# A layer of a Trainium2 kernel: projecting one batch's tokens at a time, normalising along the free axis, then transposing, in place of projecting head by head and summing squares with matmuls

## The reference, cut to what matters

```python
def _rmsnorm(x, w):
    var = jnp.mean(xf * xf, axis=-1, keepdims=True)
    return (xf * jax.lax.rsqrt(var + EPS)).astype(x.dtype) * w
q = (hidden_states @ Wq.T).reshape(bsz, q_len, H, HD).transpose(0, 2, 1, 3)
k = (cross_attention_states @ Wk.T).reshape(bsz, kv_len, KVH, HD).transpose(0, 2, 1, 3)
v = (cross_attention_states @ Wv.T).reshape(bsz, kv_len, KVH, HD).transpose(0, 2, 1, 3)
q = _rmsnorm(q, q_norm_w)
...
k = _rmsnorm(k, k_norm_w)
scores = jnp.einsum('bhqd,bhkd->bhqk', q, k) * scale
scores = scores + attention_mask[:, :, :, :kv_len]
probs = jax.nn.softmax(scores.astype(jnp.float32), axis=-1).astype(q.dtype)
out = jnp.einsum('bhqk,bhkd->bhqd', probs, v)
return out @ Wo.T
```

## Time and profile before

| | us |
|---|---|
| median of 3 runs (1788.86 to 1794.28) | 1790.83 |
| the profiled execution's own time | 1788.83 |
| its span, first to last instruction | 1787.0 |
| busy in the span: PE / DVE / POOL / ACT | 1642.3 / 1172.7 / 1053.3 / 811.2 |

### The profile page before, as it was taken

One profiled execution on the slowest core, in us unless ns is written; L12 is line 12 of the kernel. 1 busy time (PEld: TensorE's weight loads), 2 busy tenths in 40 slices (PEclk: granted clock), 3 DMA queues, 4 the chain that ended last, 5 costly groups with the idle time before them and its releaser, 6 DMA issues. The chain is left out here.

```text
span 1787.0 us, 26495 instructions
## 1 busy us (share of the span) xinstructions
PE 1642.3 (92%) x8578; PEld 1366.5 (76%) x8578; DVE 1172.7 (66%) x2367; ACT 811.2 (45%) x2584; POOL 1053.3 (59%) x1090
## 2 busy tenths in 40 slices
PE   6499974899999999999999999999999999996896
PEld 5377852688888888887888788888888888885684
DVE  4277757477777777666778765565755556555684
ACT  4297822344444444443444444444544444443442
POOL 6544411466666778665667676555766676653362
PEclk9699986999999999999999999999999999999895
DMA  6532100222222222212112231222222322220100
GB/s 214 148 67 45 43 1 11 66 65 66 65 60 60 72 73 77 55 57 60 53 54 69 69 95 60 62 63 59 75 74 82 84 78 80 80 66 8 59 25 24
DMA packets 73705, 117.22 MB, mean 66 GB/s; under 512 B 9633, under 2 KB 21281, under 8 KB 73569
## 3 DMA queue, kind: packets, MB, share of 16 engines
q1 hardware_dynamic: 73344, 115.26, 22.6%
q10 hardware_dynamic: 224, 0.26, 0.1%
HBM read 108.15 MB, written 7.34 MB: 65 GB/s over the span
## 5 line engine op out<-in xcount | busy, mean ns | idle before, releaser
L1156 POOL TENSOR_TENSOR a_probs<-a_probs,a_total 128x512 f32<-128x512 f32 x128 | 135.3, 1057 | 210.1 <-DVE a_total L1580 208.9
L62 POOL TENSOR_TENSOR a_w_lo<-k_ring,a_w_hi 128x512 fp32r<-128x512 f32 x186 | 240.5, 1293 | 14.9
L47 PE MATMUL ps<-a_wo_hi,a_oT_lo 128*128 128x512 f32 x512 | 211.9, 414 | 5.5 <-DVE a_oT_lo L62 3.9
L47 PE MATMUL ps<-k_xT_hi,a_w_lo 128*128 128x512 f32 x512 | 204.7, 400 | 5.6 <-DVE a_w_lo L62 5.6
L49 PE MATMUL ps<-k_xT_hi,a_w_hi 128*128 128x512 f32 x512 | 203.8, 398 | 0.0
L48 PE MATMUL ps<-k_xT_lo,a_w_hi 128*128 128x512 f32 x512 | 203.7, 398 | 0.0
L49 PE MATMUL ps<-a_wo_hi,a_oT_hi 128*128 128x512 f32 x512 | 201.1, 393 | 0.0
L48 PE MATMUL ps<-a_wo_lo,a_oT_hi 128*128 128x512 f32 x512 | 199.6, 390 | 0.0
L1417 ACT ACTIVATE a_v_hi<-ps 128x128 fp32r<-128x128 f32 x128 | 35.5, 278 | 359.2 <-PE ps L1265 359.2
L62 POOL TENSOR_TENSOR a_wo_lo<-k_ring,a_wo_hi 128x512 fp32r<-128x512 f32 x128 | 165.5, 1293 | 10.2
L1555 DVE TENSOR_TENSOR a_cross<-ps,a_cross 128x512 f32<-128x512 f32 x128 | 88.1, 688 | 120.0 <-ACT a_cross L1403 117.5
(11 more groups left out here) (398 smaller groups left out, 4598.0 us busy)
## 6 DMA issues: line engine op xcount, KB each, us to landing
k_ring<-in_L_wq SPq DMA_DIRECT2D x132, 256.0 KB, 2.6
k_ring<-in_L_wo SPq DMA_DIRECT2D x128, 256.0 KB, 2.6
k_ring<-in_L_wkv SPq DMA_DIRECT2D x66, 256.0 KB, 2.6
h_q_stack<-q_part SPq DMA_DIRECT2D x24, 256.0 KB, 4.3
k_ring<-in_L_main SPq DMA_DIRECT2D x12, 256.0 KB, 3.1
p_c_raw<-in_cT SPq DMA_DIRECT2D x4, 512.0 KB, 5.6
x<-in_x SPq DMA_DIRECT2D x8, 256.0 KB, 7.8
q_part<-p_part_hi SPq DMA_DIRECT2D x8, 256.0 KB, 2.6
```

What stands on the lines that cost most here:

```text
L47: pe.matmul(out, lhs_lo, rhs_hi, start=start, stop=False)
L62: return eng.tensor_tensor(out_lo, value, hi.bitcast(F32), ALU.subtract)
L1156: pool.tensor_tensor(heads(probs[:, :]), heads(probs[:, :]), along_last(total[:, :], S), ALU.mult).then_inc(s["probs"], 1)
```

## The change

L1 projects **rows**: one batch's 128 tokens at a time, with the tokens as the stationary operand and the weights as the moving one. `project_rows(m)` does 12 matmuls of 512 columns (the four query heads of the group, into one bank of PSUM) and 12 of 256 columns (value and key head, into half a bank). The sum of squares is then along the free axis. ACT squares key and queries at once (640 columns), DVE sums them to five numbers a token and adds epsilon, POOL takes the power of 128x5, DVE multiplies the five heads by their scales, and PE turns the five heads (`turn_heads`), from where ACT and DVE split them for the score matmuls. The values come out with tokens on the partitions, so `values` and its transpose go for L1. `sums`, the spreading matmul, `add_mask` and the rest of the cross-partition norm go. The mask is added to one part of the scores by a single DVE instruction (`mask_scores`), which takes the place of ACT's copy of that part (`take_cross`).

L1's rows run three steps ahead of the items (ROW_LOOK); the loops begin at step -3. A unit's weights stay for its four rows: the Q chunks live in `qT`, which L1 no longer needs for queries, and K and V come interleaved in two chunks kept in a weight ring of five places. All six first chunks are split by ACT and DVE at step -3. L2 keeps its old form; its first eight heads are projected in steps 61 to 65 (`projects_of_step`). The second half of the feed-forward layer begins one step later. The values have three buffers in place of two. The weights are laid out for this on the host, and a DMA scratch size of 1024 is asked for.

The core of the diff (left out: names, semaphores, places of tiles, waits on freed places, the shift of L2's counters):

```diff
+def projects_of_step(T):
+
+    first = LAYER_ITEMS
+    early = {first - 3: (0, 1), first - 2: (2, 3), first - 1: (4, 5), first: (6,), first + 1: (7,)}
+    if T in early:
+        return [first + n for n in early[T]]
+    return [T + LOOK] if first + 1 < T < ITEMS - LOOK else []
...
+    if r == 0:
+        before, after = [("K", v + 1, 1), ("O", v, 2)], [("O", v, 3)]
+    elif r == 1:
+        before, after = [("Q", v + 2, 0), ("Q", v + 2, 1)], []
+    elif r == 2:
+        before, after = [("Q", v + 2, 2), ("Q", v + 2, 3)], []
+    else:
+        before, after = [("K", v + 2, 0), ("O", v + 1, 0), ("O", v + 1, 1)], []
...
+    between = {
+        57: ([("K", first, 0)], []), 58: ([("Q", first, 0)], [("Q", first, 1)]),
+        59: ([("O", last, 0)], [("O", last, 1)]), 60: ([("O", last, 2)], [("O", last, 3)]),
+        61: ([], [("Q", first, 2), ("Q", first, 3)]), 62: ([("V", first, 0)], [("K", second, 0), ("Q", second, 0)]),
+        63: ([("Q", second, 1), ("O", first, 0)], [("O", first, 1)]), 64: ([("Q", second, 2), ("O", first, 2)], [("O", first, 3)]),
+        65: ([("Q", second, 3), ("V", second, 0)], [("K", second + 1, 0)])}
...
+    extra = {21: [("S", 0, 0)], 22: [("U", 0, 0)], 29: [("M", 0, 0), ("M", 0, 1)], 30: [("M", 0, 2)], 31: [("M", 0, 3)],
+             61: [("M", 1, 0)], 62: [("M", 1, 1)], 63: [("M", 1, 2)], 64: [("M", 1, 3)]}
...
+            def row_scales(m):
+                pool.wait_ge(s["veps"], m + 1)
+                pool.tensor_tensor(scales[:, :], scales[:, :], C.neg_half[:, 0:HEADS], ALU.pow).then_inc(s["scale"], 1)
...
+            for T in range(START, ITEMS + 1):
+                if is_row(T + 2):
+                    row_scales(T + 2)
...
-                if 0 <= P - 1 < LAYER_ITEMS:
-                    if (P - 1) % HQ == 0:
-                        key_scales((P - 1) // HQ)
-                    query_scales(P - 1)
                 if is_item(T + 1):
                     normalise(T + 1)
                 for c in after:
...
+            def project_rows(m):
+
+                u, j = m // UNIT, m % UNIT
+                rows_x = [tuple(head(x, j) for x in pair) for pair in tokens(R_[half_of(u)])]
+                rows_c = [tuple(head(x, j) for x in pair) for pair in context_tokens(half_of(u))]
+                wait_from_one(pe, s["normed"], m)
+                for k in range(KT):
+                    if j == 0:
+                        chunk_ready(pe, ("Q", u, k))
+                    last = matmul_split(pe, bank_q, rows_x[k], home(("Q", u, k)), k == 0, k == KT - 1)
+                last.then_inc(s["q_mm"], 1)
+                wait_from_one(pe, s["kT_lo"], m)
+                for k in range(KT):
+                    if j == 0 and k % 2 == 0:
+                        chunk_ready(pe, ("K", u, k // 2))
+                    both = tuple(head(x, k % 2, VK) for x in home(("K", u, k // 2)))
+                    last = matmul_split(pe, bank_vk, rows_c[k], both, k == 0, k == KT - 1)
+                last.then_inc(s["vk_mm"], 1)
+
+            def turn_heads(m):
+
+                pe.wait_ge(s["normed"], m + 1)
+                wait_from_one(pe, s["pT_lo"], m - 1)
+                pe.wait_ge(s["v_lo"], m + 1)
+                for h in range(HQ):
+                    pe.transpose(head(bank_pT, h), head(rows, 1 + h), C.ident[:, :])
+                pe.transpose(bank_kT, head(rows, 0), C.ident[:, :]).then_inc(s["turned"], 1)
...
+            for t in range(START, ITEMS + 1):
                 if is_item(t + 1):
                     scores(t + 1)
                 if is_item(t):
                     turn(t)
                 if is_item(t - 1):
                     project_out(t - 1)
-                if 0 <= P - 1 < LAYER_ITEMS:
-                    sums(P - 1, t + 1)
-                if is_item(t + 1):
+                if is_item(t + 1) and not normed(t + 1):
                     values(t + 1)
                 if is_item(t):
                     mix(t)
-                if is_item(P):
+                if is_row(t + 2):
+                    turn_heads(t + 2)
+                if is_row(t + 3):
+                    project_rows(t + 3)
+                for P in projects_of_step(t):
                     project(P)
...
+            def square_rows(m):
+
+                act.wait_ge(s["q_mm"], m + 1)
+                act.wait_ge(s["vk_mm"], m + 1)
+                wait_from_one(act, s["turned"], m)
+                act.activation(rows[:, :], bank_rows, ACT.Square).then_inc(s["squares"], 1)
+
+            def round_queries(m):
+                act.activation(q_item[m % 2][0][:, :], bank_pT, ACT.Copy).then_inc(s["q_hi"], 1)
...
+            def sum_squares(m):
+
+                dve.wait_ge(s["squares"], m + 1)
+                dve.tensor_reduce(scales[:, :], by_head(rows[:, :]), AX.X, ALU.add).then_inc(s["square_sum"], 1)
+                dve.wait_ge(s["square_sum"], m + 1)
+                dve.tensor_scalar(scales[:, :], scales[:, :], HD * QK_EPS, None, ALU.add).then_inc(s["veps"], 1)
+
+            def scale_rows(m):
+
+                dve.wait_ge(s["scale"], m + 1)
+                dve.wait_ge(s["v_lo"], m + 1)
+                dve.tensor_tensor(by_head(rows[:, :]), by_head(bank_rows), along_last(scales[:, :], HD), ALU.mult).then_inc(s["normed"], 1)
...
+                if is_row(t + 2):
+                    sum_squares(t + 2)
                 if is_item(t + 1):
-                    sum_scores(t + 1)
+                    if normed(t + 1):
+                        mask_scores(t + 1)
+                    else:
+                        sum_scores(t + 1)
                 if is_item(t):
                     split_pT(t)
+                if is_row(t + 2):
+                    low_values(t + 2)
+                    scale_rows(t + 2)
                 if is_item(t + 1):
                     if normed(t + 1):
-                        add_mask(t + 1)
+                        sum_scores(t + 1)
                     maximum(t + 1)
...
+                if is_row(t + 2):
+                    low_keys(t + 2)
+                    low_queries(t + 2)
                 if is_item(t + 1):
                     invert(t + 1)
```

More of the change, by code:

```diff
@@ L939, in chunks_of_step @@
         before, after = [("Q", v + 2, 2), ("O", v + 1, 0)], [("O", v + 1, 1)]
[L940 to L948 removed]
+    columns_first = [[c for c in part if 0 <= c[1] < UNITS] for part in (before, after)]
+    first, second = last + 1, last + 2
+    between = {
[4 more added lines that the diff above has]
+        65: ([("Q", second, 3), ("V", second, 0)], [("K", second + 1, 0)])}
+    before, after = between[T] if T in between else rows_first if T < LAYER_ITEMS else columns_first
+    before, after = list(before), list(after)
+    extra = {21: [("S", 0, 0)], 22: [("U", 0, 0)], 29: [("M", 0, 0), ("M", 0, 1)], 30: [("M", 0, 2)], 31: [("M", 0, 3)],
+             61: [("M", 1, 0)], 62: [("M", 1, 1)], 63: [("M", 1, 2)], 64: [("M", 1, 3)]}
+    after += extra.get(T, [])
     if T in (97, 99, 101, 103):
```

367 lines of the change are left out of this document (167 added, 200 removed).

## The result

The changed kernel takes 1729.12 us (median of 4 runs, 1727.99 to 1734.99), the kernel before 1792.55 us beside it (4 runs, 1788.86 to 1799.53). The ratio is 0.9645, with a 95% interval of 0.9625 to 0.9665. A second set of runs gave 1730.55 us and 0.9638 (0.9611 to 0.9665). The forecast was 1742, in a range of 1727 to 1774: right in direction and mechanism, and 11 to 13 us too slow.

What follows compares the result with a forecast made beforehand. The prediction took PE's own instructions to bound L1. From the profiled 1788.8 us, - 53 - 12 + 4 + 3 + 9 = 1740, plus 2.0 for the median, gave 1742 us, range 1727 to 1774 (forecast's own 1727 to 1757).

Steps and rivals of the forecast that it cites:

- The bound: L1 is bound by PE's own instructions: PE busy 314 of 320 us; forecast with PE still the bound, chance 0.62.
- 38.5 to 39.5: Sign in the changed profile: units of L1 without feed-forward pieces lie this many us apart.
- PE's work, -53: PE in L1: 5.35 us a unit leave, 2.0 come, net 3.3 less in 16 units, 53 us less.
- dear 256 columns: Rival, PE's row projections: a 256-column matmul costs 0.17 us, giving 1780 us; chance 0.05.
- transposes in series: Rival, PE's five transposes a row: they don't overlap, 1.1 us more each row, giving 1812 us; chance 0.02.
- The chain under PE: Row's norm, from projection's end (T0) to scaled rows: done 0.2 to 0.6 us before PE reaches `turn_heads` at 4.83.
- Waits that go, -12: PE's waits in L1 at `turn`, `project_out` and `sums`, caused by late DVE masking, go: 12 us less.
- The start, +4 (0 to +10): Start of L1: PE waits 4.2, 3.3 and about 2 us at the first three `turn_heads`, net 4 us more.
- The seam, +3: Seam to L2, step 62: second query head waits 1.5 us for its bank; with its like elsewhere, 3 us more.
- Late steps, +9: Eight to ten steps with feed-forward pieces or extra chunks: POOL's power or DVE's reduction 1 to 2 us late.
- The rivals that ended slower than before (0.07): POOL late with the power in every step, 1826 us, chance 0.05; transposes that don't overlap, 1812 us, chance 0.02.

Runs made afterwards that it cites:

- e_turns_twice: The changed kernel with the five transposes of an item's heads done twice into the same places: 1763.37 us, ratio 0.9839.
- e_one_mask_before: The kernel before with one VectorE instruction adding the mask in place of four that scale by the query's factor and add it: 1782.51 us, ratio 0.9932.
- e_power_twice: The changed kernel with GpSimd doing the power of an item's five sums twice, first into a spare tile: 1770.56 us, ratio 0.9876.
- e_delay128: The changed kernel with a VectorE copy of 128 columns put ahead of the scaling of an item's rows: 1734.09 us, ratio 0.9678.
- e_power_late: The changed kernel with GpSimd's power put behind the first weight chunk of its step instead of ahead of it: 1756.59 us, ratio 0.9791.
- e_fewer_sums: The kernel before with fewer, four-column matmuls for the norm's sums and a spreading matmul of 128 columns instead of 512: 1755.14 us, ratio 0.9782.

## Why the prediction was right, and by which terms it was off

**The bound.** Right. PE is busy 279 of 280 us, and the transposes that e_turns_twice adds to PE alone come through in full. The unit, 38.05 us, lies a little below the 38.5 to 39.5 that the prediction gave as its sign; its own step of 9.58 makes 38.3.

**PE's work, -53.** Right in its net, by two errors that cancel. A unit of the changed kernel is 38.05 us with next to no waits, one of before without its waits 41.44 (e_one_mask_before): 3.4 us a unit, forecast 3.3. I had read `scores` as 0.93 us from one step. In the changed kernel they take 0.86 (508.62 to 509.48), and they did in many steps of before: my unit of 41.7 was 0.3 too long, and my step of 9.58 0.07 too long. Five transposes (0.46 for 0.45) and twelve matmuls of 256 columns (4 x 0.36 = 1.44) came out as priced; the rivals of dear 256 columns and of transposes in series fall with that.

**The chain under PE.** Right step by step: squares 0.24 behind T0 (0.20), the reduction at 0.97 (0.95, given as 1.0), the power at 2.08 (2.1), scaled at 4.3 (4.1 to 4.5), slack 0.43 (0.2 to 0.6; the prediction's own 4.83 less 4.1 to 4.5 is 0.3 to 0.7, from which it must have taken a hand-over of 0.1); e_power_twice and e_delay128 bear out a slack of some 0.4.

**Waits that go, -12.** Right: 12 us in e_one_mask_before (8.8 by its marks), of which its trace shows 7 as waits from 380 us on; in the changed kernel none of the 12.5 us of before in that stretch is left, and 3.3 of other kinds have come.

**The start, +4 (0 to +10).** Right, a little small. The waits inside the start, from the second matmul group to the first `mix`, are 2.4 + 5.0 + 3.2 + 1.8 + 0.2 = 12.5 us. Before had 2.4 + 1.5, two of 0.3 and 0.5 for weights, and these two, together 7.0:

```profile
326.01 1.05 PE L1230 MATMUL ps<-ones,a_squares 128*128 128x1 f32 x8 [1.18 <-ACT a_squares L1392]
332.01 1.05 PE L1230 MATMUL ps<-ones,a_squares 128*128 128x1 f32 x8 [1.18 <-ACT a_squares L1392]
```

That is +5.5 in waits. The lower granted clock of the start (0.75 for 0.89) comes on top, and no run prices it. For the first three `turn_heads` I had 4.2, 3.3 and 2; they are 5.0, 3.2 and 0.2, so that part holds. What I had left out is the 2.4 us before the second group of weights is there and the 1.8 us of the first `mix`; on the side of before I had counted 5.4 for 7.0.

**The seam, +3.** One wait of 1.66 us at 977.53, as worked out (1.5); its likes did not come.

**Late steps, +9.** This is the term that failed. I supposed eight to ten steps in which extra chunks or feed-forward pieces make POOL's power or VectorE's reduction 1 to 2 us late. The trace has 1.0 us of such waits in three places. The reason is in the rows: GpSimd stands idle 2.4 us ahead of the power in half of the steps of a plain unit, and a step with feed-forward pieces is longer on PE too, so that the others have more time in it. e_power_late shows the other side: with that idle time used up, one step in four is late.

With the measured terms the sum is 1788.8 - 54 - 12.5 + 5.5 + 1.7 + 1.0 + 0.6 (other waits from 380 us on) = 1731, beside 1735.0 and 1731.7 in the two profiled executions. I had then added 2 us for the median; it lay 1 to 6 below them instead. The agreement can't be closer than a few us: from `turn(127)` to the end, where none of the experiments' edits runs, the traces take 146.0 to 153.2 us.

What the sum has left out: from `turn(68)` to `turn(127)`, in L2, the changed kernel and its variants need 1.6 to 3.5 us more than before (541.4). Some 1.7 of it lies between `turn(68)` and `turn(88)` in all of them, where the feed-forward pieces of the second half come one step later; no run took this apart. The other 1.6 stands in some traces only, in one step: in the first trace `turn(126)` to `turn(127)` takes 8.4 us for 6.8, with a granted clock of 0.62 from 1576 to 1580 us, and 1.00 in the same step of before. PE's waits on the probabilities are the same in that stretch, 9.2 us.

**The range.** 1727 follows from the low ends of the new waits; their high ends (10 + 12 + 15 for 16) give 1763, not the 1757 of the text. Nothing hangs on it.

The rivals that ended slower than before (0.07) were GpSimd and the transposes. The one variant that does turn slower is none of them: it is the one with four masking instructions on VectorE, at +107 us.

## What to carry to other kernels

When one engine is busy 98% of a stage, price an edit in that engine's start-to-start distances, and then check each chain that the edit makes against the time at which that engine comes to it; here both worked to about 0.1 us. Read a price from several steps, not one, and before you put a lump sum on "steps that will be late", look at the idle time ahead of the instruction that is to be late. The value of relief on a secondary engine depends on what stands behind it in its queue: taking out four masking instructions for one gave 12 us in one order of work, and putting four back cost 107 in the other.

## What the runs showed of the hardware that I had not expected

- **A matmul of float32 with one output column was no cheaper than one with four.** Four of one column (eight instructions) take 0.81 us to the next instruction's start, 0.20 each; one of four columns (two instructions) takes 0.13. The first row is of e_fewer_sums, and the transpose starts behind the sums:

```profile
540.26 0.28 PE L1229 MATMUL ps<-ones,a_squares 128*128 128x4 f32 x2
540.39 0.31 PE L1263 MATMUL ps<-ident,a_vT 128*128 128x128 f32 x1
```

- **In these traces GpSimd slowed VectorE only where both of VectorE's tensor operands lie in SBUF** (the on-chip memory of the tiles; PSUM is the one that the matmuls write). The four masking instructions of before take 1.13 us in a step in which GpSimd is idle meanwhile (548.2 to 553.3), and 3.77 where it subtracts beside them. The changed kernel's mask is added to scores in PSUM, and averages 0.691 us over 64 steps (0.693 at most), with GpSimd busy beside it for more than half of each. In e_one_mask_before, where the one instruction reads scores and mask from SBUF, it takes 0.68 us with GpSimd idle and up to 1.80 beside it. Two rows of before, and the group of the changed kernel (count | busy us, mean ns | idle before):

```profile
550.32 1.13 DVE L1564 SCALAR_TENSOR_TENSOR a_probs<-a_cross,a_q_scale,k_mask 128x128 f32<-128x128 f32 x4
...
571.20 3.77 DVE L1564 SCALAR_TENSOR_TENSOR a_probs<-a_cross,a_q_scale,k_mask 128x128 f32<-128x128 f32 x4
```
```profile
L1609 DVE TENSOR_TENSOR a_cross<-ps,k_mask 128x512 f32<-128x512 f32 x64 | 44.2, 691 | 8.1 <-PE ps L1308 8.1
```
